# Attention units reordered: scores, transposes in 64-row pieces, context, and the next pair's projections in one block of every fifth unit

## The chip, the cores and the metric

The kernel runs on one core of one Trainium2 chip. The metric is the time of the whole program on the device in microseconds (us), less is better. The core has five engines that work side by side, each through its own instructions in order: PE (TensorE, matrix products and transposes; its weight loads are listed apart as PEld), DVE (VectorE), ACT (ScalarE), POOL (GpSimd) and SP (SyncE, which here only issues DMA transfers). They wait for each other through counting semaphores.

## The reference

Two layers of a graph network over 625 nodes of width 512. What the change touches is multi-head attention with 8 heads of width 64, which occurs three times: once in the expert block of layer 0 (`att0`, no mask, biases on q, k and v) and twice in layer 1 (`att1`, `att2`, masked by the graph's adjacency, a bias on q alone). Cut to what matters, with the head dimension first:

```
q, k, v = heads(x @ Wq + bq), heads(x @ Wk + bk), heads(x @ Wv + bv)   # each (8, 625, 64)
s = q @ k.T * 64 ** -0.5                                               # (8, 625, 625)
p = softmax(where(edge, s, -inf))                                      # att0: no mask
out = (p @ v) @ Wo + bo
```

Around them lie graph aggregation by one-hot products, a linear-attention mixer in each layer, an 8-expert feed-forward block with routed tokens, and batch and layer norms. All of it is fp32.

## The kernel before

**Tiles.** The 625 rows are 5 chunks of 125 (`NC`, `NP`). The 8 heads are 4 pairs (`PAIRS`), and the two heads of a pair lie side by side on 128 partitions of qT and kT, 64 each. One attention is therefore 20 units `u = 5 * i + c`: pair `i`, query chunk `c`.

**The work of one unit.** On PE: `scores(u)` (line 828) multiplies 125 queries by all 625 keys for each head, with 64 contraction rows, so that the two heads use different halves of the array's rows. The result lies in PSUM banks 0 to 2. `turned(u)` (lines 841 and 848) transposes the probabilities of each head in five full 125x125 pieces: four per head into bank 3 or 4 (line 841), and the fifth of both heads into bank 5 (line 848). `context(u)` (line 859) multiplies 64 columns of v per head by the turned probabilities, five chunks accumulated, with the two heads in different halves of the array's columns; it lands in the upper half of bank 5. On DVE: `largest(u)` (line 1622) adds the mask and takes the row minimum of the negated scores for each head, `scaled(u)` (lines 1630 to 1635) inverts the sums and scales both heads' exponentials, `context_out(u)` (line 1642) copies the context. On ACT: `exponentials(u)` (line 1233), one per head with its sum, and `turned_out(u)` (lines 1241 and 1245), which copies the transposes out of PSUM into the array `PT`, two pieces of 500 columns and one of 250.

**Projections.** Each pair of heads needs six (`projection(i, n)`): n = 0 to 3 are the halves of qT and kT (line 805, two passes over 312 or 313 columns for each of 4 contraction chunks), n = 4 and 5 are v for three and for two row chunks (line 810). They alternate between banks 6 and 7, and each waits until ACT (`projected`, lines 1222 to 1227) or DVE (`values`, lines 1610 and 1612) has emptied its bank. SP loads the weights of pair `i` (lines 385 to 389) when pair `i - 1`'s projections are done.

**Order.** It is written out by hand in one loop over `u` on each engine. PE in step u: `scores(u + 2)`, then the projections of the next pair that are listed for `c`, namely `((0, 1), (2,), (3,), (4,), (5,))[c]`, then `context(u - 1)`, then `turned(u)`. In the last two steps a piece of the product that follows the attention (`early`) stands ahead of the context. ACT in step u: `turned_out(u - 1)`, `exponentials(u + 2)`, then the `projected` copies. DVE in step u: `scaled(u + 1)`, `largest(u + 2)`, `values` when c is 3 or 4, `context_out(u - 1)`. The semaphores of an attention are `score`, `max`, `exp`, `prob`, `pT` (transposes done, three a unit), `pTc` (copied out, three a unit), `av` and `ctx` (context done, and copied), `proj`, `qk` and `vc` (projections done, and copied).

**Elsewhere.** `window_ranges` (line 351) reads the loop bounds of the graph's one-hot windows into registers of PE and of DVE. `gateW` and `gateW1` are two small arrays of gate weights with a zeroed margin that POOL writes at the start (lines 516 and 517).

## Time and profile before

| | |
|---|---|
| three runs | 1136.33, 1137.46, 1140.64 us; median 1137.46 |
| profiled execution | span 1134.8 us from its first to its last instruction; its time by the device's clock is not listed beside it, so the 2.7 us from the span to the median of the runs are taken as what lies around it |
| PE | busy 1087.0 us, 96% of the span |
| DVE, ACT, POOL | 560.2, 371.2 and 126.9 us, 49%, 33% and 11% |
| granted TensorE clock | 1.00 of full speed in the whole span |
| chain that ended last | PE 84%, DMA 5%, DVE 5%, issue 2%, ACT 2% |

The page of the profile gives the busy time of each engine, the chain of work that ended last (followed back from the last instruction, at each step to what released it), and groups of instructions by line. An instruction `125*64 125x125` on PE has 125 contraction rows, 64 columns of weights and 125 moving columns. An fp32 product is recorded as two matmuls (two passes), a transpose as one. Matmuls overlap, so the mean duration of one is longer than the distance between two.

### The profile page before, as it was taken

Reading aid. Unit: us, or ns where it says so; the run is one execution under the profiler, and the core shown is the slowest. Engines: PE = TensorE matmul, PEld = TensorE weight load, DVE = VectorE, ACT = ScalarE, POOL = GpSimd, SP = SyncE. Lnnn points to the kernel's source line nnn. Section 1 sums busy time; section 2 is a strip of 40 time slices with the busy share of each in tenths; the row PEclk is TensorE's granted clock in tenths of the full one; section 3 lists DMA queues with packets and bytes.
Section 4 is the critical chain, followed back from the end, with each engine's and each line's share of the span. In section 5 each row is a group of like instructions: output and inputs, shape, how many; then the busy total and the mean of one; then the engine's idle time right before and its main releaser. Section 6 shows DMA issues by size and latency. Waiting matters only on the chain.

```text
span 1134.8 us, 20059 instructions
## 1 busy us (share of the span) xinstructions
PE 1087.0 (96%) x7339; PEld 728.6 (64%) x7340; DVE 560.2 (49%) x1409; ACT 371.2 (33%) x931; POOL 126.9 (11%) x183
## 2 busy tenths in 40 slices
PE   3899999999999988999999899999999999999999
PEld 2588646468777554455545577887577778755764
DVE  7999738645445421121211444553324455587641
ACT  1012212035555412122212445453124455412630
POOL 1045460020000020010101530000000000001000
PEclk9999999999999999999999999999999999999999
DMA  4100475000000379800899840000210100000001
GB/s 133 38 1 3 131 201 213 1 28 29 19 11 1 155 248 409 332 14 18 330 400 403 295 167 29 29 29 1 75 56 29 29 29 1 1 37 1 1 3 43
DMA packets 21402, 112.69 MB, mean 99 GB/s; under 512 B 5127, under 2 KB 6904, under 8 KB 15198
## 3 DMA queue, kind: packets, MB, share of 16 engines
q1 hardware_dynamic: 15864, 100.95, 23.7%
q0 software_dynamic: 5472, 10.83, 3.6%
q8 instruction: 45, 0.74, 0.3%
q14 instruction: 21, 0.17, 0.1%
HBM read 102.78 MB, written 8.98 MB: 98 GB/s over the span
## 4 chain that ended last, share of the span: by engine, by line
PE 84%; DMA 5%; DVE 5%; issue 2%; ACT 2%; POOL 1%; DVEq 1%; SPq 0%; POOLq 0%
PE psum L624 11%; PE psum L805 10%; PE psum L1002 7%; PE psum L979 6%; PE psum L828 6%; PE psum L692 6%; PE psum L859 6%; PE psum L810 5%; PE psum L841 5%; PE psum L1129 3%; PE psum L1033 3%; DMA arena<-in_moeW 3%; PE psum L642 3%; PE psum L1107 3%; PE psum L762 2%
## 5 line engine op out<-in xcount | busy, mean ns | idle before, releaser
L624 PE MATMUL psum<-arena 128*125 128x512 f32 x320 | 140.0, 593 | 0.8 <-ACT arena L1203 0.7
L1233 ACT ACTIVATE arena<-arena,small 125x625 f32<-125x625 f32 x120 | 97.0, 809 | 89.9 <-DVE small L1622 89.9
L805 PE MATMUL psum<-arena 128*128 128x313 f32 (+1 forms) x384 | 110.0, 435 | 2.3 <-ACT arena L1171 1.4
L1308 ACT ACTIVATE arena<-psum,cols 128x64 f32<-128x64 f32 x224 | 47.4, 358 | 183.3 <-PE psum L988 183.3
L624 PEld LDWEIGHTS psum<-arena 128*125 128x125 f32 x320 | 59.2, 187 | 73.7 <-issue 69.6
L979 PE MATMUL psum<-arena 128*64 128x512 f32 x448 | 99.2, 594 | 6.1 <-DMA arena<-in_moeW 4.4
L1002 PE MATMUL psum<-arena 128*64 128x256 f32 x896 | 100.4, 381 | 3.0 <-DMA arena<-in_moeW 2.9
L805 PEld LDWEIGHTS psum<-arena 128*128 128x128 f32 x384 | 69.9, 189 | 31.2 <-ACT arena L1171 2.5
L1622 DVE CUSTOM_DVE_ANT_0 arena<-psum,cnt_adj 125x625 f32<-125x625 f32 x80 | 61.5, 806 | 55.0 <-PE psum L828 55.0
L1241 ACT ACTIVATE arena<-psum 125x500 f32<-125x500 f32 x120 | 63.8, 583 | 73.2 <-PE psum L841 73.2
L1002 PEld LDWEIGHTS psum<-arena 128*64 128x64 f32 x896 | 63.1, 137 | 36.3 <-issue 4.5
L828 PE MATMUL psum<-arena 64*125 64x113 f32 x480 | 80.3, 453 | 0.0
L859 PE MATMUL psum<-arena 125*64 125x125 f32 x1200 | 77.4, 274 | 0.5
L1516 DVE TENSOR_SCALAR arena<-arena 125x628 bf16<-125x628 f16 x222 | 76.1, 419 | 1.0 <-PE psum L682 0.6
L692 PE MATMUL psum<-arena 125*128 x1110 | 71.9, 220 | 4.1 <-DVE arena L1516 1.4
L859 PEld LDWEIGHTS psum<-arena 125*64 125x64 f32 x1200 | 63.2, 136 | 18.6 <-issue 13.1
L979 PEld LDWEIGHTS psum<-arena 128*64 128x64 f32 x448 | 31.7, 137 | 65.7 <-issue 58.3
L692 PEld LDWEIGHTS psum<-arena 125*128 125x128 bf16 x1110 | 62.2, 98 | 12.3 <-issue 10.7
L828 PEld LDWEIGHTS psum<-arena 64*125 64x125 f32 x480 | 52.5, 183 | 24.9 <-issue 16.1
L841 PE MATMUL psum<-ident,arena 125*125 125x125 f32 x480 | 67.9, 284 | 0.0
L841 PEld LDWEIGHTS psum<-ident,arena 125*125 125x125 f32 x480 | 57.1, 188 | 10.0 <-issue 9.5
L1642 DVE COPY arena<-psum 128x125 f32<-128x125 f32 x60 | 17.2, 286 | 91.7 <-PE psum L859 91.7
(299 smaller groups left out, 1422.2 us busy)
## 6 DMA issues: line engine op xcount, KB each, us to landing
arena<-in_moeW SPq DMA_DIRECT2D x32, 2048.0 KB, 18.2
arena<-in_att SPq DMA_DIRECT2D x36, 256.0 KB, 2.7
arena<-in_l1W SPq DMA_DIRECT2D x2, 2048.0 KB, 11.2
token_rows<-arena POOLq DMA_DIRECT2D x19, 128.0 KB, 4.9
rows<-in_rows SPq DMA_DIRECT2D x1, 2240.0 KB
expert_rows<-arena POOLq DMA_DIRECT2D x17, 128.0 KB, 4.8
arena<-in_gnnWo SPq DMA_DIRECT2D x2, 1024.0 KB, 5.6
arena<-token_rows POOLq DMA_DIRECT2D x14, 128.0 KB, 6.8
```

Source lines behind the costliest of these rows:

```text
L624: mm = pe.matmul(bank(b, NP, D), srcT[:, k, c * NP:(c + 1) * NP], w[:, k, :], start=(k == 0), stop=(k == KC - 1))
L692: mm = pe.matmul(psum[:, o + c * P:o + (c + 1) * P], one_src[:, s, c * NP:c * NP + P], hot_dst[:, bass.ds(e * P, P)], start=False, stop=False,
L805: mm = pe.matmul(bank(b, P, width), aw[:, w, k, :], srcT[:, k, o:o + width], start=(k == 0), stop=(k == KC - 1))
L828: mm = pe.matmul(psum[0:NP, at_:at_ + n], q[h * HD:(h + 1) * HD, c * NP:(c + 1) * NP], k[h * HD:(h + 1) * HD, o:o + n], start=True, stop=True)
L841: mm = pe.transpose(bank(3 + h, NP, NP, NP * j), Sx[u % 3][h][:, j * NP:(j + 1) * NP], ident[0:NP, 0:NP])
L859: mm = pe.matmul(psum[h * HD:(h + 1) * HD, 5 * 512 + 256:5 * 512 + 256 + NP], vv[i % 2][:, j, h * HD:(h + 1) * HD], PT[:, u % 2 * NC + j, ...
L979: mm = pe.matmul(psum[q * TT:(q + 1) * TT, 512 * b:512 * b + D], xsT[:, k4, :], EW1[par][:, k4, o:o + D], start=(k4 == 0), stop=(k4 == KC ...
L1002: mm = pe.matmul(psum[q * TT:(q + 1) * TT, 4 * 512:4 * 512 + D // 2], hT[:, f, :], EW2[par][:, f, q * (D // 2):(q + 1) * (D // 2)], start= ...
L1233: act.activation(Sx[u % 3][h], Sx[u % 3][h], ACT.Exp, bias=small[0:NP, 80 + n:81 + n], scale=-1.0, accum_out=small[0:NP, 120 + n:121 + n]) ...
L1241: act.activation(PT[:, u % 2 * NC:u % 2 * NC + 4, h * NP:(h + 1) * NP], bank(3 + h, NP, 4 * NP).rearrange("p (j n) -> p j n", j=4), ACT.Co ...
L1516: ve.tensor_scalar(one_src[:, s, :], iota_src[:, 0:SW], float(1024 * w), key[:, bass.ds(e, 1)], ALU.add, ALU.is_equal).then_inc(hot_ready, 1)
L1622: ve.tensor_tensor_reduce(Sx[u % 3][h], psum[0:NP, o:o + N], mask, 1.0, NO_EDGE / 10, ALU.add, ALU.min, small[0:NP, 80 + n:81 + n]).then_i ...
```

## The change

On PE step u becomes: `scores(u + 2)`; `turned(u)`; in the step with `c == 2` all six projections of the next pair in a row; `context(u - 1)`. The last two units (`u >= LAST`, 18 and 19) keep their transposes at the end of the step. Each full transpose becomes two pieces, one of contraction rows 0 to 63 and one of rows 64 to 124, which go to different PSUM banks: rows 0 to 63 of both heads to bank 3, rows 64 to 124 to bank 4, and the fifth pieces to bank 7 (bank 5 for the last two units). The pieces alternate between the two halves of the array's rows; where both halves write to one bank, a new semaphore `low` holds the later ones back. A unit has 20 pieces instead of 10 transposes. `context` now waits itself for the copy of the context before it.

On ACT step u becomes `turned_out(u)`, `exponentials(u + 2)`, and in the step with `c == 2` the four `projected`. The copies go by row half (488 and 512 columns) and not by head, and the last one is 256 columns wide. On DVE both `values` stand in the step with `c == 2`, behind `largest(u + 2)`. `PT` grows from 250 to 256 columns a chunk. Outside the attention, the two gate arrays become one, and each bound that `window_ranges` reads is masked with 4095. The call sites pass the engine as well. The arena grows by 16 columns.

```diff
@@ -30,6 +30,7 @@
 KG = -(-ET // GT)
 TP = ET + GT - 1
 DW = 32
+END_BITS = 4095
 NW = -(-N // DW)
...
@@ -44,6 +45,19 @@
 ASCALE = HD ** -0.5
 HALF = [(0, 312), (312, 313)]
 PART = [(0, 2 * NP), (2 * NP, 3 * NP)]
+QROWS = [(0, 64), (64, NP)]
+LAST = PAIRS * NC - 2
+BLOCK = 2
+
+
+def blocks_before(u):
+
+    return min(PAIRS, 1 + (u + NC - 1 - BLOCK) // NC)
+
+
+def tails_bank(u):
+
+    return 7 if u < LAST else 5
 WMIN = 64
...
@@ -142,15 +156,15 @@
         upper = sb("upper", [NP, NP])
         twos = sb("twos", [EX, NP])
         b2rows = sb("b2rows", [EX, D])
-        gateW = sb("gateW", [P, KC * EX + WMIN])
-        gateW1 = sb("gateW1", [P, KC * EX + WMIN])
+        gates = sb("gates", [P, 2 * KC * EX + WMIN])
+        gateW, gateW1 = gates[:, 0:KC * EX + WMIN], gates[:, KC * EX:]
         ffW1 = sb("ffW1", [P, KC, F1])
         ffW2 = sb("ffW2", [P, D])
...
@@ -232,8 +246,8 @@
         o_s = o_v + 2 * NC * P
         Sx = [[at(o_s + (2 * u + h) * N, NP, N) for h in range(2)] for u in range(3)]
         o_p = o_s + 6 * N
-        PT = at(o_p, NP, 2 * NC, 2 * NP)
-        assert o_p + 4 * NC * NP <= AR - 3 * KC * P
+        PT = at(o_p, NP, 2 * NC, 2 * P)
+        assert o_p + 4 * NC * P <= AR - 3 * KC * P
         lnc = [at(o_M + i * N, NP, N) for i in range(2)]
...
@@ -311,7 +325,7 @@
         A = []
         for a in range(3):
             A.append({n: sem(f"att{a}_{n}") for n in (
-                "wq", "wk", "wv", "proj", "qk", "vc", "tail", "score", "max", "exp", "sum", "prob", "pT", "pTc",
+                "wq", "wk", "wv", "proj", "qk", "vc", "tail", "score", "max", "exp", "sum", "prob", "low", "pT", "pTc",
                 "av", "ctx")})
         gates_ready, slots_ready, scattered, zero_rows = (
...
@@ -348,12 +362,12 @@
         row = lambda name: rows[:, ROWS[name], :]
 
 
-        def window_ranges(engine):
+        def window_ranges(eng, engine):
             first, second = [nc.values_load_multi_w_load_instructions(
                 bounds[0:1, o:o + NW], engines=[engine], min_val=-NW * KG * GT, max_val=NW * KG * GT,
                 skip_runtime_bounds_check_because="the program clamps a window's first tile and its count")[1]
                 for o in (0, NW)]
-            return [0] + list(first), second
+            return [0] + [end & END_BITS for end in first], second
 
         @block.sync
...
@@ -513,8 +527,9 @@
             pool.memset(zero_bf, 0.0).then_inc(consts, 1)
             pool.memset(small[:, 612:613], 1.0e-15)
             pool.memset(twos[:], 2.0).then_inc(consts, 1)
-            pool.memset(gateW[:, KC * EX:], 0.0).then_inc(consts, 1)
-            pool.memset(gateW1[:, KC * EX:], 0.0).then_inc(consts, 1)
+            for h in range(2):
+                o = 2 * KC * EX + h * (WMIN // 2)
+                pool.memset(gates[:, o:o + WMIN // 2], 0.0).then_inc(consts, 1)
             pool.memset(zero_rows_sb, 0.0).then_inc(consts, 1)
             head_blocks(HD, consts, 15)
...
@@ -833,20 +848,38 @@
 
                 def turned(u):
 
-                    for h in range(2):
-                        pe.wait_ge(s["prob"], 2 * u + h + 1)
-                        if u:
-                            pe.wait_ge(s["pTc"], 3 * (u - 1) + h + 1)
-                        for j in range(4):
-                            mm = pe.transpose(bank(3 + h, NP, NP, NP * j), Sx[u % 3][h][:, j * NP:(j + 1) * NP],
-                                              ident[0:NP, 0:NP])
-                        mm.then_inc(s["pT"], 1)
+                    def piece(g, h, j):
+                        r0, r1 = QROWS[g]
+                        o = 512 * (3 + g) + 64 * (4 * h + j) if j < 4 else 512 * tails_bank(u) + 64 * (2 * h + g)
+                        return pe.transpose(psum[0:NP, o:o + r1 - r0], Sx[u % 3][h][r0:r1, j * NP:(j + 1) * NP],
+                                            ident[r0:r1, r0:r1])
+
+                    pe.wait_ge(s["prob"], 2 * u + 1)
+                    if u:
+                        pe.wait_ge(s["pTc"], 3 * (u - 1) + 2)
+                    for j in range(4):
+                        piece(0, 0, j)
+                        piece(1, 0, j)
+                    pe.wait_ge(s["prob"], 2 * u + 2)
                     if u:
                         pe.wait_ge(s["pTc"], 3 * u)
+                    if u < LAST:
+                        pe.wait_ge(s["vc"], 2 * blocks_before(u))
+                    else:
                         pe.wait_ge(s["ctx"], u)
-                    for h in range(2):
-                        mm = pe.transpose(bank(5, NP, NP, NP * h), Sx[u % 3][h][:, 4 * NP:N], ident[0:NP, 0:NP])
-                    mm.then_inc(s["pT"], 1)
+                    piece(0, 0, 4)
+                    piece(1, 1, 0)
+                    piece(0, 1, 4).then_inc(s["low"], 1)
+                    piece(1, 1, 1)
+                    piece(0, 1, 0)
+                    piece(1, 1, 2)
+                    piece(0, 1, 1)
+                    piece(1, 1, 3).then_inc(s["pT"], 1)
+                    piece(0, 1, 2)
+                    pe.wait_ge(s["low"], u + 1)
+                    piece(1, 0, 4)
+                    piece(0, 1, 3).then_inc(s["pT"], 1)
+                    piece(1, 1, 4).then_inc(s["pT"], 1)
 
                 def context(u):
 
@@ -854,11 +887,13 @@
                     pe.wait_ge(s["pTc"], 3 * u + 3)
                     if c == 0:
                         pe.wait_ge(s["vc"], 2 * i + 2)
+                    if u:
+                        pe.wait_ge(s["ctx"], u)
                     for j in range(NC):
                         for h in range(2):
                             mm = pe.matmul(psum[h * HD:(h + 1) * HD, 5 * 512 + 256:5 * 512 + 256 + NP],
                                            vv[i % 2][:, j, h * HD:(h + 1) * HD],
-                                           PT[:, u % 2 * NC + j, h * NP:(h + 1) * NP],
+                                           PT[:, u % 2 * NC + j, h * P:h * P + NP],
                                            start=(j == 0), stop=(j == NC - 1))
                     mm.then_inc(s["av"], 1)
 
@@ -877,15 +912,20 @@
                     i, c = divmod(u, NC)
                     if u + 2 < PAIRS * NC:
                         scores(u + 2)
-                    if i + 1 < PAIRS:
-                        for n in ((0, 1), (2,), (3,), (4,), (5,))[c]:
+                    if u < LAST:
+                        turned(u)
+                    if c == BLOCK and i + 1 < PAIRS:
+                        for n in range(6):
+                            if n == 1:
+                                pe.wait_ge(s["pTc"], 3 * (u + 1))
                             projection(i + 1, n)
-                    if u >= PAIRS * NC - 2:
+                    if u >= LAST:
                         pe.wait_ge(s["vc"], 2 * PAIRS)
-                        early(u - (PAIRS * NC - 2), s["ctx"])
+                        early(u - LAST, s["ctx"])
                     if u:
                         context(u - 1)
-                    turned(u)
+                    if u >= LAST:
+                        turned(u)
                 pe.wait_ge(s["max"], 2 * PAIRS * NC)
                 early(2, s["ctx"])
                 context(PAIRS * NC - 1)
@@ -1236,13 +1276,14 @@
                 def turned_out(u):
                     if u >= 2:
                         act.wait_ge(s["av"], u - 1)
-                    for h in range(2):
-                        act.wait_ge(s["pT"], 3 * u + h + 1)
-                        act.activation(PT[:, u % 2 * NC:u % 2 * NC + 4, h * NP:(h + 1) * NP],
-                                       bank(3 + h, NP, 4 * NP).rearrange("p (j n) -> p j n", j=4),
+                    slot = u % 2 * NC
+                    for g in (1, 0):
+                        act.wait_ge(s["pT"], 3 * u + (1 if g else 3))
+                        n = QROWS[g][1] - QROWS[g][0]
+                        act.activation(PT[:, slot:slot + 4, :].rearrange("p j (h g n) -> p h j g n", h=2, g=2)[:, :, :, g, 0:n],
+                                       bank(3 + g, NP, 512).rearrange("p (h j n) -> p h j n", h=2, j=4)[:, :, :, 0:n],
                                        ACT.Copy).then_inc(s["pTc"], 1)
-                    act.wait_ge(s["pT"], 3 * u + 3)
-                    act.activation(PT[:, u % 2 * NC + 4, :], bank(5, NP, 2 * NP), ACT.Copy).then_inc(s["pTc"], 1)
+                    act.activation(PT[:, slot + 4, :], bank(tails_bank(u), NP, 2 * P), ACT.Copy).then_inc(s["pTc"], 1)
 
                 act.activation(small[0:1, 95 + a:96 + a], onesf[0:1, 0:1], ACT.Exp)
                 for n in range(4):
@@ -1251,14 +1292,16 @@
                 exponentials(1)
                 for u in range(PAIRS * NC):
                     i, c = divmod(u, NC)
-                    if u >= PAIRS * NC - 2:
+                    if u >= LAST:
                         early(u - (PAIRS * NC - 1))
-                    if u:
+                    if u < LAST:
+                        turned_out(u)
+                    elif u > LAST:
                         turned_out(u - 1)
                     if u + 2 < PAIRS * NC:
                         exponentials(u + 2)
-                    if i + 1 < PAIRS:
-                        for n in ((0, 1), (2,), (3,), (), ())[c]:
+                    if c == BLOCK and i + 1 < PAIRS:
+                        for n in range(4):
                             projected(i + 1, n)
                 early(1)
                 turned_out(PAIRS * NC - 1)
...
@@ -1653,8 +1696,9 @@
                         scaled(u + 1)
                     if u + 2 < PAIRS * NC:
                         largest(u + 2)
-                    if i + 1 < PAIRS and c >= 3:
-                        values(i + 1, c + 1)
+                    if c == BLOCK and i + 1 < PAIRS:
+                        values(i + 1, 4)
+                        values(i + 1, 5)
                     if u >= PAIRS * NC - 2:
                         early(u - (PAIRS * NC - 2))
                     if u:

```

## Rows read from the trace of the kernel before

**Rows 1.** The page: span, busy time by engine, the chain by engine

```profile
span 1134.8 us, 20059 instructions
...
PE 1087.0 (96%) x7339; PEld 728.6 (64%) x7340; DVE 560.2 (49%) x1409; ACT 371.2 (33%) x931; POOL 126.9 (11%) x183
...
PE 84%; DMA 5%; DVE 5%; issue 2%; ACT 2%; POOL 1%; DVEq 1%; SPq 0%; POOLq 0%
```

**Rows 2.** Chain of waits in the second attention: start us, us, what

```profile
665.37 1.26 PE psum L828 x6
...
696.62 1.26 PE psum L828 x6
...
697.88 4.41 PE psum L805 x16
...
704.58 0.22 PE psum L848 x2
...
706.06 2.31 PE psum L805 x8
...
708.37 1.22 PE psum L859 x20
...
715.67 1.07 PE psum L841 x8
...
718.22 2.84 PE psum L810 x24
...
724.82 1.96 PE psum L810 x16
...
729.28 1.26 PE psum L828 x6
```

**Rows 3.** Timeline of units without projections: start us, us, engine line op

```profile
767.17 0.80 DVE L1622 CUSTOM_DVE_ANT_0 arena<-psum,cnt_adj 125x625 f32<-125x625 f32 x1
...
767.90 0.80 DVE L1622 CUSTOM_DVE_ANT_0 arena<-psum,cnt_adj 125x625 f32<-125x625 f32 x1
...
768.02 0.82 ACT L1233 ACTIVATE arena<-arena,small 125x625 f32<-125x625 f32 x1 [0.98 <-DVE small L1622]
...
769.59 1.34 PE L828 MATMUL psum<-arena 64*125 64x113 f32 x8
...
769.63 1.04 ACT L1241 ACTIVATE arena<-psum 125x500 f32<-125x500 f32 x2
...
769.76 0.17 DVE L1630 TENSOR_SCALAR small<-small 125x2 f32<-125x2 f32 x1 [0.85 <-ACT arena L1233]
...
770.57 0.37 ACT L1245 ACTIVATE arena<-psum 125x250 f32<-125x250 f32 x1
...
771.08 0.80 DVE L1622 CUSTOM_DVE_ANT_0 arena<-psum,cnt_adj 125x625 f32<-125x625 f32 x1
```

**Rows 4.** Instructions by line and form: count, busy us, mean ns, idle before

```profile
L841 PEld LDWEIGHTS psum<-ident,arena 125*125 125x125 f32 x480 | 57.1, 188 | 10.0 <-issue 9.5
...
L828 PEld LDWEIGHTS psum<-arena 64*125 64x125 f32 x480 | 52.5, 183 | 24.9 <-issue 16.1
...
L988 PEld LDWEIGHTS psum<-ident,arena 128*128 128x128 f32 x112 | 11.7, 140 | 12.3 <-issue 11.4
...
L841 PE MATMUL psum<-ident,arena 125*125 125x125 f32 x480 | 67.9, 284 | 0.0
...
L963 PE MATMUL psum<-ident,arena 64*128 64x64 f32 x56 | 6.1, 229 | 0.0
...
L692 PE MATMUL psum<-arena 125*128 x1110 | 71.9, 220 | 4.1 <-DVE arena L1516 1.4 <-issue 0.2
```

**Rows 5.** Timeline of PE: products and transposes with 64 moving columns

```profile
398.85 4.68 PE L946 MATMUL psum<-arena 125*128 125x64 f32 x40 [0.59 <-DVE arena L1736]
...
415.34 0.44 PE L963 MATMUL psum<-ident,arena 64*128 64x64 f32 x4
```

**Rows 6.** The page: DMA issues, KB each, us from issue to landing

```profile
arena<-in_att SPq DMA_DIRECT2D x36, 256.0 KB, 2.7
```

More of the change, by code:

```diff
@@ L152, in build @@
         EW1_SIZE = KC * FF
-        AR = EW1_SIZE + 30893
+        AR = EW1_SIZE + 30909
         arena = sb("arena", [P, AR])
@@ L668, in _ @@
             pe.wait_ge(range_ready, 1)
-            ends, shifts = window_ranges(mybir.EngineType.PE)
+            ends, shifts = window_ranges(pe, mybir.EngineType.PE)
             def window_banks(w):
@@ L1508, in _ @@
             ve.wait_ge(range_ready, 1)
-            ends, shifts = window_ranges(mybir.EngineType.DVE)
+            ends, shifts = window_ranges(ve, mybir.EngineType.DVE)
             for w in range(NW):
```

## The prediction

> **What bounds the kernel now.** I read the page first. TensorE is busy for 96% of the span and holds 84% of the chain that ended last [rows 1], so what counts is how long PE takes for an attention, and whether it ever has to wait there. Next the chain of waits through the second attention, where the reader should see an almost unbroken row of PE blocks. From it comes the make-up of one unit. The blocks of 24 and of 16 records of line 810 differ by 0.88 us for 8 records, 0.11 each, and 0.20 is left over in each block; line 805 gives 2.10 us for 8 records (0.2625 each) and 0.21 over [rows 2]. The transposes (1.07 for 8, then 0.22 for 2 more) are 0.11 each and 0.19 over; the two that follow without a change of shape carry nothing extra. So each change of the array's tiling costs about 0.2 us: the array runs empty, and the first weight load is not hidden. A unit without projections is 1.26 (scores) + 1.22 (context) + 1.07 + 0.22 = 3.77 us, five of them 18.9, and the projections of a pair are 4.41 + 2.31 + 2.31 + 2.84 + 1.96 = 13.8, together 32.7; the chain has 729.28 - 696.62 = 32.66 for a pair [rows 2]. With projections in every unit PE alone sets the pace (6.5 us a unit), and DVE and ACT have much slack.
>
> Last I read the timeline of the units of the fourth pair, which have no projections. There the pace is no longer PE's. `largest` starts at 767.17 and again at 771.08, 3.91 us apart, though PE needs 3.77. The reader should follow the loop: the first head's minimum (767.17) lets ACT start its exponentials (768.02), both are done for DVE's line 1630 at 769.76, and the scaling ends when the next `largest` starts at 771.08 [rows 3]. This loop of 0.85 + 1.74 + 1.32 us is already the limit wherever projections are missing. The change creates many such units.
>
> **The change, part by part.** Count in one attention the stretch from scores(2) to scores(19): 665.37 to 769.59, 104.2 us [rows 2, 3], 17 steps.
>
> *Scores next to transposes.* Both use 64 contraction rows and 125 columns, so the tiling does not change between them; 0.19 us per unit goes away, if the pieces themselves take as long as before.
>
> *The pieces.* 20 pieces of half the rows in two alternating halves of the array are 10 slots. What is one slot? Moving columns fall from 125 to 64 or 61, but each piece still loads 125 columns of weights. A load of 125 columns lasts 183 ns with 64 rows and 188 with 125 rows [rows 4], so halving the rows saves nothing. And products with only 64 moving columns but a full load go at (4.68 - 0.28) / 39 = 0.113 us each [rows 5], the load's pace. Against this stand the four 64-row transposes of line 963, (0.44 - 0.23) / 3 = 0.07 apart [rows 4, 5]; but they have 128 weight columns, and transposes with 128 columns show a load of 140 ns where those with 125 show 188 [rows 4]. The pieces have 125. I take 0.11 a slot, nearest in width; the bounds are 0.07, and 0.22 if the halves do not overlap. Ten slots are 1.10, the same as the ten transposes without their 0.19.
> The Trainium skill ("TensorE: Matmul & The Clock Gate", LDWEIGHTS) says that a weight load takes its columns divided by 1.2 GHz whatever the contraction rows; by that rule the slot is about 0.104 us and the splitting itself earns nothing. The trace agrees: 183 against 188 ns [rows 4].
>
> *PE work per unit* is then 1.26 + 1.10 + 1.22 = 3.58 us instead of 3.77.
>
> *The block.* 32 records of line 805 (8.40), 40 of line 810 (4.40) and one change of tiling (0.20) are 13.0 us instead of 13.83, 0.83 saved per pair. Inside it nothing should wait: product 1 waits for the tail copy of the next-to-be-read transposes, about 1.4 us after they end, while product 0 lasts 2.1; product 2 waits for `projected(0)`, which ACT does after `turned_out(u)` and both exponentials (1.3 + 1.7 us), and product 1 ends 4.4 us after the block began. Weights: SP issues pair i+1's when pair i's block ends, some 16 us before use, and they land in 2.7 us [rows 6], so SP's move costs nothing; if that cover were gone, 2.7 us a pair.
>
> *The cost of bunching.* DVE stands in `values` until the block ends, and `scaled` and `context_out` behind it stand with it; ACT is done early. Neither can run ahead, because scores are only two units ahead. After the block they must do 4 units at their own pace. And the pace gets worse than 3.91, since ACT now copies unit u's transposes before the exponentials of u+2, and those transposes stand behind scores(u+2) on PE. The new loop spans two units. From the end of the minima of unit u+1: hand-over 0.05; scores until the transposes may start 1.16 (1.26 less the half of the 0.20 that lies behind them); 8 of 10 slots 0.88, and 0.2 until ACT sees them (a record of 0.28 [rows 4] less one slot, plus a hand-over); ACT's three copies 1.31 (769.63 to 770.57 + 0.37); the exponentials 1.74; inversion and scaling 1.32; both minima 1.53 (0.73 from the first to the second, then 0.80), then scores(u+4) may go [rows 3]. The sum is 8.2 us for two units, 4.1 a unit, against 3.58 of PE. This also replaces the 3.77 to 3.91 of the last pair's units.
>
> *The sum.* Of the 17 steps three hold a block: 3 x (13.0 + 3.58) = 49.7. The other 14 run at 4.11: 57.5. Together 107.3 us against 104.2, +3.1 an attention; the first unit after a block can go at PE's own 3.58, but the loop takes it back in the next, since it bounds two units together. Three attentions give +9.2 us.
>
> *Small edits.* The 0.19 saved in the last two units' transposes: nothing, they keep their order. Masks on 20 window bounds on PE and DVE: no row shows one; the nearest is PE's whole idle time before line 692, 4.1 us [rows 4]; between nothing and that, I take nothing, as the queues run ahead of a window's products. Gate arrays joined: POOL at 11% [rows 1], nothing. The wait on `low`, three slots (0.33) after the piece that it waits for, whose record lasts 0.23 to 0.28 [rows 4]: nothing to 0.05 a unit, 2.7 us in all; I take nothing. Copies of 488 + 512 + 256 columns instead of 1250: same.
>
> The profiled span of 1134.8 becomes 1144.0; the median lies 2.7 us over that span, so the forecast is 1137.5 + 9.2 = 1146.7.
>
> **The rivals.** *PE stays the bound (faster).* If the two-unit loop is shorter than reckoned, because the copies overlap the scores of the next unit or ACT gets its transposes sooner, PE runs without a wait: 3 x 13.0 + 17 x 3.58 = 99.9, -4.4 an attention, -13.1 in all, 1124.4. It decides where the loop falls below 7.2 us. For it: PE waits almost nowhere today. Against: the 3.91 us loop of [rows 3] does not depend on PE and alone already exceeds 3.58.
>
> *Fast pieces (no change).* At 0.07 a slot PE's unit is 3.18, but the loop loses only 8 x 0.04, 3.95 a unit: 39.0 + 3 x 3.18 + 14 x 3.95 = 103.8, -0.4 an attention, 1136.2. For it: line 963. Against: its 128 columns.
> The Trainium skill ("TensorEngine Tiling (Array Packing)", Theoretical Speedup) promises up to twice the speed when the contraction is at most 64 rows, since the tiles work independently; no row here shows it for loads of 125 columns, and its best case is 0.055 a slot.
>
> *Halves do not overlap (much slower).* 20 x 0.11 makes PE's unit 4.68 and the stretch 118.6 us, +43 in all, 1180. For it: 20 instructions for 10. Against: the scores of both heads run in such halves, 1.26 us for two heads of 625 columns and two passes, which at 0.2625 per 313 columns would take 2.1 one after the other [rows 2].
>
> *That it does not do what it says:* the order is plain in the loops of all three engines, and I give it no chance of its own.
>
> **How the numbers follow.** About 0.5%, 5.7 us, is what a measurement of this kernel can tell from no change. The bunched loop (forecast): 0.60, of which 0.12 ends less than 5.7 us up. PE stays the bound: 0.16, all faster. Fast pieces: 0.18, of which 0.03 faster through a shorter loop as well. No overlap: 0.06, slower. That gives faster 0.19, same 0.12 + 0.15 = 0.27, slower 0.48 + 0.06 = 0.54. The range leaves out the last case and part of the second: 1127 (PE bound in most units) to 1155 (the forecast with all of `low` and of the masks, 2.7 + 4.1, and some more). The forecast's own range is 1140 to 1154.
>
> **What would show it.** In the profile after: the chain at the scores with fixed gaps gone before the transposes, blocks of 72 projection records in about 13.0 us, pairs of pieces 0.11 us apart; PE idle before line 828 released by DVE's line 1622, about 10 us an attention, where today there is next to none; periods between scores of 3.6 and 4.6, then 3.9 and 4.3 us, between blocks; the loads of the pieces near 183 ns. Loads near 140 and slots of 0.07 would make the third case; no idle time on PE the second. I would be wrong in the step of the loop if ACT's copies start before eight slots are done or if scores wait for something other than the minima.

## The result and the profile after

The kernel after takes 1160.3 us (median of 4 runs) where the kernel before beside it takes 1139.0: a ratio of 1.018, interval 1.0156 to 1.0204. Measured again with more runs it was 1.0155 (1.0125 to 1.0186; 1157.7 against 1141.6). Each ratio and interval here and below is that of a kernel's runs to runs of the kernel before beside them. It is slower by 16 to 21 us; the forecast said slower by 9.

The page of the profile after, against [rows 1]:

```profile
span 1162.2 us, 21365 instructions
...
PE 1087.5 (94%) x7939; PEld 749.8 (65%) x7940; DVE 557.9 (48%) x1409; ACT 371.2 (32%) x931; POOL 118.2 (10%) x183
...
PEclk9999999999999989999999989999998999999999
...
PE 76%; DVE 8%; ACT 6%; DMA 5%; issue 4%; POOL 1%; DVEq 0%; SPq 0%; ACTq 0%; POOLq 0%
...
L843 PE MATMUL psum<-arena 64*125 64x113 f32 x480 | 83.8, 469 | 22.7 <-DVE small L1665 22.7
```

PE now holds 76% of the chain instead of 84%, DVE 8% instead of 5% and ACT 6% instead of 2%. PE waits 22.7 us before the scores (line 843 in this kernel), always for DVE's minima (line 1665). The granted clock shows three slices of 8 where it was 9 throughout. Behind them are four stretches at half the clock, 1.2 GHz, of 6.8 us each: one near the start of each attention (259.9, 683.1 and 891.4 us) and one in the expert block (427.1 us). That of the first attention is split over two slices and does not show.

The forms of line 854, the pieces, against [rows 4]:

```profile
L854 PE MATMUL psum<-ident,arena 61*125 61x61 f32 x600 | 79.2, 277 | 0.0
...
L854 PEld LDWEIGHTS psum<-ident,arena 64*125 64x125 f32 x600 | 77.5, 192 | 4.5 <-issue 2.3 <-DVE arena L1678 0.9
```

A piece's weight load lasts 192 ns, like the 188 of the full transposes, and not 140. The mean includes the loads at half clock; in e2 below, where the attentions have the full clock, it is 183 to 184. The chain shows the rest. Start us, us, what, for the stretch of the second attention between two blocks, and the block:

```profile
706.75 1.26 PE psum L843 x6
708.01 0.85 PE psum L854 x15
...
708.95 1.07 ACT arena L1283 x2
710.01 0.27 ACT arena L1286
710.29 1.59 ACT arena L1273 x4
...
711.91 0.18 DVE small L1673
...
713.31 0.72 DVE arena L1665
714.03 0.72 DVE arena L1665
...
714.91 1.33 PE psum L843 x6
...
723.04 1.33 PE psum L843 x6
724.38 1.09 PE psum L854 x19
725.47 8.62 PE psum L820 x32
734.08 4.40 PE psum L825 x40
738.48 1.22 PE psum L894 x20
```

The chain goes from the scores through most of the pieces to ACT's copies (lines 1283 and 1286), the exponentials (1273), DVE's inversion and scaling (1673), the minima (1665) and back to the scores: 706.75 to 714.91 to 723.04, 8.16 and 8.13 us for two units. Where [rows 2] was an unbroken row of PE blocks, PE is on this chain for about a quarter of it. The pieces take 1.09 for ten slots. Their change of tiling is gone: a unit in which PE does not wait takes 3.57 us from scores to scores in PE's timeline (739.62 to 743.20), 0.20 less than the 3.77 of the kernel before. The block is 8.62 + 4.40 = 13.0 us.

**Where the 27.4 us between the two profiled spans lie.** Each length is the difference between first matmuls of scores or contexts in PE's timeline. "Stretch" is from scores(2) to scores(19), "end" from scores(19) to the start of the last matmul of the attention's last context. The last column goes on from there to the first scores of the second attention. All lengths in us; the nine experiments stand beside, for the next section.

```
                        first      stretch                 end                     after att. 1
                        scores(0)  att 1   att 2   att 3   att 1   att 2   att 3   to att. 2
before                  243.2      104.28  104.29  104.29  20.85   15.01   15.01   282.3
after                   247.1      110.24  110.11  110.12  21.87   16.11   16.11   284.9
e1 masks                244.8      104.28  104.29  104.28  20.83   15.01   15.01   283.6
e2 pieces, old order    244.6      103.45  103.45  103.44  22.36   15.90   15.90   284.9
e3 filled start         244.5      107.38  107.38  107.37  21.87   16.10   16.10   286.9
e4 block alone          245.3      109.01  106.99  108.91  20.83   15.01   15.01   287.1
e5 e3 + full tail       245.5      107.36  107.36  107.36  20.62   15.66   15.65   281.9
e6 e3 + copy order      244.5      106.53  106.53  106.53  22.21   16.38   16.36   285.9
e7 projections moved    244.5      101.58  101.58  101.58  20.83   15.01   15.03   282.9
e8 block filled         245.2      106.31  106.32  106.32  20.82   15.01   15.00   283.1
e9 after again          244.5      108.68  108.67  110.25  21.87   16.11   16.11   282.3
```

Of the 27.4 us the three stretches hold 17.6, the three ends 3.2, the start 3.9 and the expert block between the first and the second attention 2.6. The stretches are 5.8 to 6.0 us longer each where the forecast had 3.1.

What is missing in them is at their beginning. PE's timeline of the second attention after, and the windows on both sides of 683.1 us (the columns are length, busy time and count by engine, clock, DMA share, GB/s):

```profile
678.81 1.34 PE L843 MATMUL psum<-arena 64*125 64x113 f32 x8
680.26 1.36 PE L854 MATMUL psum<-ident,arena 64*125 64x64 f32 x20
683.48 2.49 PE L843 MATMUL psum<-arena 64*125 64x113 f32 x8 [1.86 <-DVE small L1665]
685.74 2.22 PE L854 MATMUL psum<-ident,arena 61*125 61x61 f32 x20
687.89 2.28 PE L894 MATMUL psum<-arena 125*64 125x125 f32 x20
690.10 1.34 PE L843 MATMUL psum<-arena 64*125 64x113 f32 x8
```

```profile
675.60:683.10 7.50, 5.91 (x53) 4.80 (x52) 6.15 (x17) 3.41 (x8) 0.49 (x1) 1.00 0.32 105
683.10:689.90 6.80, 6.42 (x48) 5.95 (x48) 3.20 (x10) 3.65 (x10) 0.00 (x0) 0.50 0.00 1
```

PE waits 1.86 us for the minima of unit 2. In the window up to 683.1 it is busy for 5.91 of 7.50 us, and then it is granted half the clock for 6.8 us: scores, pieces and context take 2.49, 2.22 and 2.28 us instead of 1.34, 1.25 and 1.29. From scores(3) to scores(4) it is 6.62 us. The same happens at 259.9 and at 891.4 us.

### The profile page after: what moved, and what is told of

Its sections match the earlier page's. It is cut to its first block, busy times and chain, and to the rows that moved or that the text cites. A ratio compares the mean times of both kernels' runs of the same rounds, so it can differ in the third digit from the quotient of the medians.

```text
span 1162.2 us, 21365 instructions
## 1 busy us (share of the span) xinstructions
PE 1087.5 (94%) x7939; PEld 749.8 (65%) x7940; DVE 557.9 (48%) x1409; ACT 371.2 (32%) x931; POOL 118.2 (10%) x183
## 4 chain that ended last, share of the span: by engine, by line
PE 76%; DVE 8%; ACT 6%; DMA 5%; issue 4%; POOL 1%; DVEq 0%; SPq 0%; ACTq 0%; POOLq 0%
PE psum L639 12%; PE psum L820 9%; PE psum L1042 7%; PE psum L1019 6%; PE psum L707 5%; PE psum L825 5%; PE psum L843 4%; PE psum L854 3%; PE psum L1073 3%; PE psum L1169 3%; PE psum L657 3%; PE psum L1147 3%; ACT arena L1273 3%; DVE arena L1665 3%; DMA arena<-in_moeW 3%
## 5 line engine op out<-in xcount | busy, mean ns | idle before, releaser
L1283 ACT ACTIVATE arena<-psum 125x488 f32<-125x488 f32 x120 | 64.0, 586 | 139.4 <-PE psum L854 139.4
L820 PE MATMUL psum<-arena 128*128 128x313 f32 (+1 forms) x384 | 105.2, 430 | 2.3 <-ACT arena L1211 1.4
L843 PE MATMUL psum<-arena 64*125 64x113 f32 x480 | 83.8, 469 | 22.7 <-DVE small L1665 22.7
L854 PEld LDWEIGHTS psum<-ident,arena 64*125 64x125 f32 (+1 forms) x1200 | 85.7, 192 | 4.5 <-issue 2.3
L854 PE MATMUL psum<-ident,arena 64*125 64x64 f32 (+1 forms) x1200 | 79.4, 274 | 1.4 <-DVE arena L1685 1.1
L894 PE MATMUL psum<-arena 125*64 125x125 f32 x1200 | 80.3, 282 | 0.0
L894 PEld LDWEIGHTS psum<-arena 125*64 125x64 f32 x1200 | 65.8, 141 | 8.2 <-issue 4.2
L1678 DVE TENSOR_SCALAR arena<-arena,small 125x625 f32<-125x625 f32 x120 | 60.0, 543 | 2.1
```

What stands on the lines that cost most here:

```text
L820: mm = pe.matmul(bank(b, P, width), aw[:, w, k, :], srcT[:, k, o:o + width], start=(k == 0), stop=(k == KC - 1))
L843: mm = pe.matmul(psum[0:NP, at_:at_ + n], q[h * HD:(h + 1) * HD, c * NP:(c + 1) * NP], k[h * HD:(h + 1) * HD, o:o + n], start=True, stop=True)
L854: return pe.transpose(psum[0:NP, o:o + r1 - r0], Sx[u % 3][h][r0:r1, j * NP:(j + 1) * NP], ident[r0:r1, r0:r1])
L894: mm = pe.matmul(psum[h * HD:(h + 1) * HD, 5 * 512 + 256:5 * 512 + 256 + NP], vv[i % 2][:, j, h * HD:(h + 1) * HD], PT[:, u % 2 * NC + j, ...
L1283: act.activation(PT[:, slot:slot + 4, :].rearrange("p j (h g n) -> p h j g n", h=2, g=2)[:, :, :, g, 0:n], bank(3 + g, NP, 512).rearrange( ...
```

## The experiments

Two questions: whether the pieces, the block or the order cost what I had reckoned, and what lowered the clock. All experiments carry the masks on the window bounds.

**e1, the masks alone.**

```diff
-            return [0] + list(first), second
+            return [0] + [end & 4095 for end in first], second
```

> The kernel before with one edit: the loop bounds that window_ranges reads are masked with 4095. Theory (the masks are what moves the start of the first attention from 243.2 to 247.1 us): scores(0) of the first attention near 247.1 us, span about 3.9 us longer, time 1142 to 1144, every stage after it as long as before. Rival (the 3.9 us come from the changed attention, the joined gate arrays or from chance): scores(0) near 243.2, time within 1 us of the kernel before.

Measured: 1141.0 against 1140.1 (ratio 1.0006, 0.9992 to 1.0021). The first scores start at 244.8, 1.6 us later than before, and nothing else moves but the expert block (1.4 longer, with 3.4 us of half clock in it). The seven profiles of e2 to e8, all with the masks, have 244.5 to 245.5, and the kernel after 247.1 once and 244.5 the second time (e9). The upper three (e4, e5 and e8, 245.2 to 245.5) have 3.4 us of half clock at 43.4 us; the others have none there. The windows' products, from the first to the last, take 77.4 us in the kernel before and 78.4 to 78.7 in all seven profiles with the masks and the full clock there. So the masks delay the first attention by some 1.3 to 1.6 us by the profiles, about 1.0 to 1.3 of it where the masked bounds are used. This rests on one profile of the kernel before; the times by themselves do not tell it from nothing, and 2.4 us is the most that the interval allows for the whole kernel. The forecast had the masks at nothing; my expectation here, 3.9, was too much.

**e2, the pieces in the old order.** The functions `turned` and `turned_out` of the kernel after, with the fifth pieces in bank 5; all loops as before. The wider `PT` and the joined gate arrays of the kernel after are in it too, and nothing moves before the attentions: the first scores are at 244.6 us, in e1 at 244.8.

> The kernel before with the masks and with the 64-row pieces, but in the old order (scores, projections spread over all units, context, transposes; fifth pieces in bank 5; ACT's copies as in the kernel after, but of unit u-1). The transposes now share their tiling with the scores that follow. Theory: a slot stays 0.11 us, a block of pieces takes 1.16 us up to the next scores where ten full transposes took 1.28, so an attention is 18 x 0.12 = 2.1 us shorter and nothing waits; 6.5 us under e1, about 1136.5, granted clock 1.00 throughout. Rival A (the pieces themselves are dear, or lower the granted clock): longer than e1, stretches of low clock at the attentions. Rival B (adjacency earns the whole 0.2 without the waits on low and on the context's copy): 10.5 us under e1.

Measured: 1141.5, ratio 1.0005 (0.9991 to 1.0018), the same as e1. The chain of one unit in the second attention:

```profile
707.89 1.37 PE psum L841 x19
709.26 1.12 PE psum L830 x6
710.38 2.31 PE psum L807 x8
712.69 1.22 PE psum L876 x20
```

DVE's copy of the context before it, in the timeline:

```profile
707.94 0.29 DVE L1660 COPY arena<-psum 128x125 f32<-128x125 f32 x1 [4.08 <-PE psum L876]
```

Pieces and scores are 2.49 where transposes and scores were 1.07 + 0.22 + 1.26 = 2.55 [rows 2]. Sharing the tiling takes 0.14 from the scores, and the pieces give back 0.07: the distance from the fourth to the fifth pair of pieces is 0.18 instead of 0.11, where they wait for the copy of the context, which ends at 708.23. At the wait on `low`, near the end of the pieces, the distance stays 0.11. A stretch is 0.84 us shorter and an end 0.89 (in the first attention 1.5) us longer, so nothing is left. There is no low clock at the attentions: the pieces do not lower it. Both rivals fall. Of my 6.5 us the stretches show 2.5, because of the wait for the context's copy and a smaller saving at the scores, and the ends, which I had left out, take those back.

**e3, PE kept busy at unit 0.**

```diff
                     if u < LAST:
                         turned(u)
+                    if u == 0:
+                        for _ in range(4):
+                            pe.matmul(bank(5, P, 256), onesf[0:NP, :], rows[:, 0, 0:256], start=True, stop=True)
```

> The kernel after, with four products of 256 columns put on PE behind the pieces of unit 0 of each attention, where PE otherwise waits 1.86 us for DVE; their results are not used. Theory (the granted clock falls at the start of each attention because PE idles there): no stretch of half clock at 256, 679 and 887 us, period from scores(3) to scores(4) near 3.9 to 4.3 instead of 6.0 to 6.6, each attention 2.3 to 2.7 us shorter, 7 to 8 us in all. Rival (the clock falls because of what the 64-row pieces are, not because PE waits): the stretches stay, the time is that of the kernel after or a little longer.

```profile
676.80 1.36 PE L854 MATMUL psum<-ident,arena 64*125 64x64 f32 x20
678.09 1.99 PE L919 MATMUL psum<-rows,onesf 125*128 125x256 f32 x8
680.02 1.34 PE L843 MATMUL psum<-arena 64*125 64x113 f32 x8
```

Measured: 1153.1, ratio 1.0099 (1.0076 to 1.0123) against 1.018 and 1.0155. The scores of unit 2 start 4.66 us behind those of unit 1, as in the kernel after, so the filling changes no time there but the clock. The clock is full in all three attentions, and each stretch is 107.38 us, 3.1 over the kernel before: the forecast's own number. (Between 396.9 and 420.8 us, in the expert block, this profile has 23.9 us of half clock; e4 has as much, and the other kernels have 3.4 to 10.2 us there, the kernel before none in its one profile. It differs from profile to profile and does not follow the change.) Filling a wait of 1.86 us with work that nobody uses makes the kernel 6 to 9 us faster, by its ratio against the two of the kernel after.

**e4, the block alone, and e8, the block with the start filled.** All else in the old order, with full transposes.

```diff
-                        for n in ((0, 1), (2,), (3,), (4,), (5,))[c]:
+                        for n in (range(6) if c == 2 else ()):
                             projection(i + 1, n)
...
-                    if i + 1 < PAIRS and c >= 3:
-                        values(i + 1, c + 1)
+                    if i + 1 < PAIRS and c == 2:
+                        values(i + 1, 4)
+                        values(i + 1, 5)
```

> The kernel before with the masks and with the projections in one block at c == 2 on PE, ACT and DVE, all else in the old order with full transposes. Theory: PE saves 0.8 us a block, but the units without projections run at the pace of the DVE-ACT loop, 3.9 us where PE needs 3.77: periods of the scores 3.8, 3.95, 3.9, 3.9 and 16.8, an attention 1 to 2 us longer, 3 to 5 us over e1, about 1147, and more if the clock falls as in the kernel after. Rival (spreading never mattered, and the loss of the kernel after comes from the new order of scores and transposes alone): an attention 2.5 us shorter, 1135.

> Kernel of e4 (old order, one block) with the same four unused products behind unit 0's transposes. Theory (e4 was the block's loss by bunching, about 1.9 us an attention, plus stretches of low clock): no low clock at the attentions, the stretch from scores(2) to scores(19) 106.0 to 106.3 us in all three, against 104.3 in e1: 5.5 to 6 us over e1, 1146. Rival (the block lowers the clock however PE's gap at the start is filled): stretches of low clock stay, 1150.

The fragment leaves out ACT's `projected`, which moves to `c == 2` in the same way. PE's timeline in e4, and the windows before and after the clock falls:

```profile
676.88 1.34 PE L828 MATMUL psum<-arena 64*125 64x113 f32 x8
678.33 1.15 PE L841 MATMUL psum<-ident,arena 125*125 125x125 f32 x8
679.31 0.38 PE L848 MATMUL psum<-ident,arena 125*125 125x125 f32 x2
681.54 2.38 PE L828 MATMUL psum<-arena 64*125 64x113 f32 x8 [1.85 <-DVE small L1622]
```

```profile
674.20:681.70 7.50, 5.55 (x42) 4.41 (x40) 6.03 (x18) 2.62 (x7) 0.00 (x0) 1.00 0.24 79
681.70:685.10 3.40, 3.40 (x20) 2.56 (x22) 2.46 (x7) 2.28 (x7) 0.00 (x0) 0.50 0.01 2
```

The same place in e8, where the products of line 891 fill the wait:

```profile
672.71 1.89 PE L891 MATMUL psum<-rows,onesf 125*128 125x256 f32 x8
674.72 1.34 PE L828 MATMUL psum<-arena 64*125 64x113 f32 x8
```

Measured: e4 1150.4 (ratio 1.0074, 1.0052 to 1.0096), e8 1148.1 (1.0070, 1.0043 to 1.0097). The clock falls in e4 at the same place behind the same wait, with full transposes, and stays up in e8. That settles its cause together with e3: the wait that the missing projections leave, not the pieces. The expectation of e4, 1147, was 3 us low, and that of e8, 1146, 2 us. In e8 every stretch is 106.3 us, 2.0 over before, with periods of 16.78, 3.77, 3.95, 3.90 and 3.90 us. So the bunching alone costs 2.0 of the 3.1 us; the DVE-ACT loop of [rows 3] is the pace of three units in five. The rival, 2.5 us shorter, is wrong.

**e5, the end with full transposes** (in e3, units 18 and 19 as in the kernel before).

> Kernel of e3 with ten full transposes instead of the pieces in the last two units of each attention, as in the kernel before. Theory (the pieces cost 1.1 us at each attention's end, because there they stand between context and the early product and bring two changes of tiling where full transposes bring one): from scores(19) to the end of the last context 15.0 us instead of 16.1, about 3.3 us under e3, ratio to the kernel before about 1.007. Rival (the end is longer because bunching left DVE and ACT behind): the stretch stays at 16.1 us.

Measured: 1150.3, ratio 1.0091 (1.0063 to 1.0119). The end of the second and third attention is 15.66 us, not 15.0: the pieces explain 0.45 of the 1.10. The other 0.65 lie at the wait that PE's timeline of this kernel shows:

```profile
779.72 1.29 PE L908 MATMUL psum<-arena 125*64 125x125 f32 x20
781.76 1.93 PE L1090 MATMUL psum<-arena 128*128 128x250 f32 x8 [0.76 <-DVE arena L1709]
```

The first `early` product needs the copy of the context that ran just before it (line 1709); in the old order the transposes lay between them. The rival, DVE and ACT left behind by the bunching, is out: e4 and e8 have the same bunching, and their ends are the 15.01 us of the kernel before.

In the first attention it is otherwise. There e5's end is 20.62 us, 0.23 less than before, so the pieces cost 1.25 us. They wait for the copy of the context before their fifth pair, in the kernel after for 0.20 us in unit 18 and for 0.85 in unit 19:

```profile
381.11 0.88 PE L854 MATMUL psum<-ident,arena 64*125 64x64 f32 x12 [0.85 <-DVE arena L1685]
```

**e6, ACT's old order of copies** (in e3; the fragment is ACT's loop).

```diff
-                    if u < LAST:
-                        turned_out(u)
-                    elif u > LAST:
-                        turned_out(u - 1)
+                    if u and not (c == BLOCK + 1 and i + 1 < PAIRS):
+                        turned_out(u - 1)
+                    if c == BLOCK and i + 1 < PAIRS:
+                        turned_out(u)
```

> Kernel of e3 with ACT's old order of copies and exponentials: turned_out(u-1) before exponentials(u+2), only in the step with the block turned_out(u) as well. Theory (the two-unit loop through scores, pieces, copies and exponentials sets 8.2 us for two units; without it only the DVE-ACT loop of 3.9 is left): periods after a block 3.6, 4.2, 3.9, 3.9 instead of 3.6, 4.7, 3.8, 4.3, the stretch from scores(2) to scores(19) 106.4 us instead of 107.4, 2 to 3 us in all. Rival (the periods of 4.7 and 4.3 come from PE's own order or from contention): they stay.

Measured: 1151.0, ratio 1.0084 (1.0055 to 1.0112), stretch 106.53. The periods after a block are 3.57, 4.16, 3.90, 3.90 in place of 3.57, 4.66, 3.81, 4.32. The two-unit loop is gone when the copies do not stand ahead of the exponentials, and the older loop of 3.9 is what is left. The stretches are 2.5 us shorter in all, the ends 0.9 us longer; the times of e3, e5 and e6 are too close to be told apart.

**e7, projections next to full transposes.** The kernel before; PE's projections move, and DVE copies the context first.

```diff
-                    if i + 1 < PAIRS:
-                        for n in ((0, 1), (2,), (3,), (4,), (5,))[c]:
-                            projection(i + 1, n)
...
                     if u:
                         context(u - 1)
+                    if i + 1 < PAIRS:
+                        for n in ((0, 1), (2,), (3,), (4,), (5,))[c]:
+                            projection(i + 1, n)
                     turned(u)
```

> The kernel before with the masks and full transposes; on PE the projections stay spread but stand between context(u-1) and turned(u) instead of ahead of the context, and DVE copies the context before the values. Projections and full transposes have the same tiling, so a unit has three changes of it and not four. Theory (a change costs 0.2 us, PE stays the bound because the projections stay spread): the 15 units with projections 0.2 us shorter each, periods 5.9 instead of 6.1, the stretch from scores(2) to scores(19) 101.5 us instead of 104.3, 8.4 us in all, about 1132, ratio 0.993, granted clock 1.00 in the attentions. Rival (the change of tiling is hidden elsewhere, or the context now waits for ACT's copies): no change from e1.

```profile
703.03 1.26 PE psum L828 x6
704.29 1.23 PE psum L859 x20
705.52 2.31 PE psum L805 x8
707.83 0.87 PE psum L841 x8
708.70 0.22 PE psum L848 x2
708.92 1.26 PE psum L828 x6
```

Measured: 1132.0 us against 1140.7, ratio 0.9936 (0.9911 to 0.9960). The eight transposes behind a projection take 0.87, eight times 0.11, instead of 1.07: the 0.20 of the change of tiling are gone, with no wait in their place. Of the 15 units that I had counted 14 gain: the step of unit 0 has no context, its projections stood next to the transposes before, and its period is 6.76 in both kernels. So the stretches are 2.7 us shorter each, 8.1 in all. This version beats both kernels.

**e9, the kernel after once more.**

> The kernel after, unchanged, beside the kernel before, for its ratio on this chip, its second profile, and the parts that the first profile left open. Theory: three stretches of low clock of 6.8 us at the start of the attentions, each 2.7 us longer from scores(3) to scores(4), are part of this kernel and come back; the start of the first attention (247.1 us in the first profile, 244.5 to 245.5 in eight others with the masks) and the expert block's low clock vary from run to run and are no part of it, so scores(0) near 245 us; ratio 1.016 to 1.019. Rival (the late start and the low clock belong together and to chance): scores(0) at 247 again, or no low clock at the attentions and a time of e3, 1153.

Measured: ratio 1.0155 (1.0125 to 1.0186). The low clock at the attentions comes back, this time for 3.4, 3.4 and 6.8 us where I had expected 6.8 three times, and costs 1.3, 1.3 and 2.9 us against the 107.38 of e3. The first scores are at 244.5 and the expert block is as long as before, so 2.6 us at the start and 2.6 us there were chance in the first profile; its PE comes to the windows' first product late already, at 45.3 us instead of 42.6. Its span of 1154.0 is 19.2 over the kernel before: 14.7 in the stretches, 3.2 in the ends, 1.3 at the start.

## Why the prediction was wrong

Its direction and its main mechanism hold, its size does not: it gave 9.2 us and a range up to 1155; measured are 1160.3 and 1157.7.

*A slot is 0.11 us.* Right. Loads of 192 ns, ten slots in 1.09. That the contraction rows do not matter to a load, as the Trainium skill says ("TensorE: Matmul & The Clock Gate", LDWEIGHTS), holds here: 192 ns with 64 rows, 188 with 125. The twofold speed that the Trainium skill allows for ("TensorEngine Tiling (Array Packing)", Theoretical Speedup) does not come here, where each piece still loads 125 columns: ten slots of pieces take the 1.09 us of ten full transposes.

*PE's unit of 3.58 and the block of 13.0.* Right: the shortest period is 3.57, and the block is 13.0 in the chain.

*The two-unit loop, +3.1 us an attention.* Right to 0.1: loop 8.2 forecast, 8.13 to 8.16 measured; periods after a block of 3.6, 4.6, 3.9 and 4.3 forecast, 3.57, 4.66, 3.81 and 4.32 measured; 3.1 forecast, 3.1 in e3, where nothing else interferes. This is not luck: read off the chain, no part of the loop is off by more than 0.15 us. e8 and e6 split it: 2.0 from bunching, and 0.85 of the remaining 1.1 goes when ACT's copies go behind. The "about 10 us" of PE's waits in an attention did not follow from the sum, which has 14 x (4.11 - 3.58) = 7.4; the page has 22.7 in three attentions, 7.6 each.

*What failed* is the sum. It took each of the 14 units without a block at 4.11 us, so it priced PE's new waits by their length alone. The first term left out is the clock: the wait of 1.86 us at unit 0, where the projections had stood, is followed by 3.4 to 6.8 us at 1.2 GHz, and the period from scores(3) to scores(4) is 5.2 to 6.6 us instead of the 3.90 of e3. That is 1.3 to 2.9 us an attention, 5.5 us in all in e9 and 8.3 in the first profile, against the 107.38 of e3. "With projections in every unit PE alone sets the pace" was written, but not what they did for the clock. The second is the step "the 0.19 saved in the last two units' transposes: nothing, they keep their order". Their own order stayed, but their neighbours changed: 1.1 us in each of the last two attentions, 0.65 for the copy that `early` now waits for and 0.45 for the pieces, and 1.0 in the first, from the pieces (e5). The third is "I take nothing" for the masks: by the profiles 1.3 to 1.6 us. With the 9.3 of the loop this makes 19 to 22 us. The two ratios give 20.5 and 17.7; the second lies under it, but its interval reaches to 21.2.

*Nothing for `low`.* Right: in the kernel after and in e2 the pieces stay 0.11 us apart across that wait. The wait that does cost is the one for the copy of the context before the fifth pair of pieces, 0.07 a unit in e2 and up to 0.85 us at the end of the kernel after's first attention, and the forecast had no term for it.

*The rivals.* None of the three came. PE did not stay the bound, there were no fast pieces, and the halves do overlap.

## What to carry to other kernels

Reordering work to save changes of the array's tiling paid here where PE stayed the bound in every unit (e7) and lost where it did not (the kernel after): put work of the same tiling side by side without bunching it, since independent work spread between dependent steps is what covers the other engines' loop. Before pricing such a loop, write out every engine's order over two units, because a copy placed ahead of the exponentials can close a loop that spans both. And price each new wait of PE twice, once as time and once as what it may do to the clock of the work behind it. That second price is a risk and not a fixed cost, as the next section shows; at the start of a phase, where nothing is ahead, look at the wait by itself.

## What the runs showed of the hardware

A wait of 1.85 to 1.86 us on PE, which was busy for 5.5 to 5.6 of the 7.5 us up to the wait's end, went with half the clock for 3.4 or 6.8 us in all nine attentions of the kernel after, e4 and e9; the clock fell between 0.4 us before that end and 1.4 us after it. It did not fall in any of the twelve attentions where PE was filled there (e3, e5, e6, e8), although in e3 PE also waits for 1.02, 0.20 and 0.68 us between two later blocks. The length varies between executions: the kernel after had 6.8 three times in one profile, and 3.4, 3.4 and 6.8 in the other.

The length of a wait and PE's busy time before it do not settle it. At 43 us (45 in the first profile of the kernel after) every profile has a wait of 2.0 to 2.2 us before line 682, or that line's counterpart, with PE busy for 5.3 to 5.5 of the 7.5 us up to its end. The clock fell there in three of the eleven profiles (e4, e5, e8). The wait in the kernel before, and the windows from 42.7 us there and from 43.4 us in e4:

```profile
42.69 0.22 PE L682 MATMUL psum<-arena 125*128 125x64 f16 x2 [2.03 <-DVE arena L1505]
```

```profile
42.70:46.10 3.40, 2.47 (x37) 2.03 (x38) 3.02 (x11) 0.00 (x0) 0.00 (x0) 1.00 0.64 265
43.40:46.80 3.40, 2.86 (x28) 2.87 (x29) 3.21 (x10) 0.00 (x0) 0.00 (x0) 0.50 0.50 210
```

Why nine of nine fell at the attentions and three of eleven here stays open.

Changes of tiling are not all alike: between projections and full transposes all of the 0.20 us went (e7), and so they did with the pieces behind the scores (the kernel after, 3.57 against 3.77). With the scores behind the pieces only 0.14 went (e2), which no run here explains.
